# Clearing a block's semaphores from GpSimd inside the next block, without the second meeting of all engines at three inner block ends

## What is computed

```
x = x + 0.5 * ffn(layernorm(x))
x = x + attn(layernorm(x))
x = x + 0.5 * ffn(layernorm(x))

def ffn(x):                          # soft mixture of experts, 16 experts with 64 slots each
    x  = layernorm(x) * g + b
    se = (layernorm(slot_embeds) * slot_g + slot_b) * scale
    logits   = einsum('bnd,esd->bnes', x, se)
    dispatch = softmax(logits, axis=1)             # over tokens
    combine  = softmax(logits over all e*s)        # over slots
    slots = einsum('bnd,bnes->besd', x, dispatch)
    gate  = gelu(slots @ Wg + bg);  up = slots @ Wu + bu
    eout  = (gate * up) @ Wd + bd
    return einsum('bns,bso->bno', combine, eout)

def attn(x):                         # linear attention inside chunks of 32 tokens
    Q, K, V = x@Wq.T, x@Wk.T, x@Wv.T
    S = einsum('bncd,bnkd->bnck', Q, K) * decay_mask
    O = einsum('bnck,bnkd->bncd', S, V)
    return sigmoid(x@Wg.T) * O @ Wo.T + x
```

## Time and profile before

| | |
|---|---|
| median of 3 runs | 1861.09 us (1861.06 to 1861.68) |
| the profiled execution, its own time | 1854.48 us |
| its span, first to last instruction | 1852.8 us |
| TensorE busy | 1800.0 us, 97% of the span, 11756 matmuls |
| VectorE, ScalarE, GpSimd busy | 71%, 63%, 45% |
| mean granted TensorE clock | 0.998 |

### The profile page before, as it was taken

The page is one execution under the profiler, slowest core; times in us unless marked ns, Lnnn a source line. Parts: engine busy times, 40 slices in busy tenths (PEclk is TensorE's granted clock), DMA queues, the critical chain, the costliest instruction groups (busy, mean ns, idle before and its releaser), DMA issues. The chain is left out here.

```text
span 1852.8 us, 35562 instructions
## 1 busy us (share of the span) xinstructions
PE 1800.0 (97%) x11756; PEld 1620.4 (87%) x11756; DVE 1309.5 (71%) x2365; ACT 1161.3 (63%) x2285; POOL 825.1 (45%) x1036
## 2 busy tenths in 40 slices
PE   6999999999999999999999999999999999999998
PEld 5788888878999999989999877888888789999998
DVE  6866666664899888855555587666565668997886
ACT  5776676675665777754444367666666755667774
POOL 3423334234788655422222134242432458885553
PEclk9999999999999999999999999999999999999999
DMA  4642443251654777712222165333323426647773
GB/s 156 233 151 100 159 158 119 108 192 36 221 195 156 254 268 267 285 47 69 68 68 68 58 238 193 120 142 147 148 102 114 159 88 230 204 173 269 262 257 146
DMA packets 106940, 297.85 MB, mean 161 GB/s; under 512 B 16784, under 2 KB 56592, under 8 KB 94544
## 3 DMA queue, kind: packets, MB, share of 16 engines
q1 hardware_dynamic: 106832, 296.49, 44.7%
HBM read 187.18 MB, written 109.28 MB: 160 GB/s over the span
## 5 line engine op out<-in xcount | busy, mean ns | idle before, releaser
L115 POOL TENSOR_TENSOR pool_carrier<-minus_half 128x1 f32<-128x1 f32 x224 | 71.7, 320 | 599.5 <-PE f2bank L984 197.6
L824 ACT ACTIVATE f2r_lt<-f2bank,slot_shift 128x512 f32<-128x512 f32 x128 | 88.3, 690 | 125.3 <-PE f2bank L955 125.2
L824 ACT ACTIVATE f1r_lt<-f1bank,slot_shift 128x512 f32<-128x512 f32 x128 | 88.3, 690 | 122.1 <-PE f1bank L955 122.0
L673 DVE TENSOR_TENSOR f2r_e_lo<-f2bank,f2r_e_hi 128x512 fp32r<-128x512 f32 x128 | 82.4, 685 | 80.6 <-ACT f2r_e_hi L905 80.6
L673 DVE TENSOR_TENSOR f1r_e_lo<-f1bank,f1r_e_hi 128x512 fp32r<-128x512 f32 x128 | 82.4, 684 | 79.7 <-ACT f1r_e_hi L905 79.7
L1685 PE MATMUL f1bank<-f1c_eo,f1c_e_hi 128*128 128x258 f32 (+1 forms) x512 | 130.6, 287 | 0.5 <-DVE f1c_xout L1591 0.4
L1685 PE MATMUL f2bank<-f2c_eo,f2c_e_hi 128*128 128x258 f32 (+1 forms) x512 | 130.0, 286 | 0.5 <-DVE f2c_xout L1591 0.4
L1686 PE MATMUL f1bank<-f1c_eo,f1c_e_hi 128*128 128x256 f32 (+1 forms) x512 | 128.2, 282 | 0.0
L1686 PE MATMUL f2bank<-f2c_eo,f2c_e_hi 128*128 128x256 f32 (+1 forms) x512 | 128.1, 282 | 0.0
L1538 POOL TENSOR_TENSOR f1c_e_lo<-f1c_lt,f1c_e_hi 128x512 fp32r<-128x512 f32 x64 | 82.7, 1294 | 76.7 <-ACT f1c_e_hi L1651 76.7
L1538 POOL TENSOR_TENSOR f2c_e_lo<-f2c_lt,f2c_e_hi 128x512 fp32r<-128x512 f32 x64 | 82.8, 1295 | 75.7 <-ACT f2c_e_hi L1651 75.7
(11 more groups left out here) (347 smaller groups left out, 6661.2 us busy)
## 6 DMA issues: line engine op xcount, KB each, us to landing
logits<-f1r_lt SPq DMA_DIRECT2D x16, 2048.0 KB, 7.3
f1c_lt<-logits SPq DMA_DIRECT2D x32, 1024.0 KB, 7.3
logits<-f2r_lt SPq DMA_DIRECT2D x16, 2048.0 KB, 7.3
f2c_lt<-logits SPq DMA_DIRECT2D x32, 1024.0 KB, 7.0
normalized<-t_xin SPq DMA_DIRECT2D x32, 512.0 KB, 2.6
t_xin<-in_L_attn_x SPq DMA_DIRECT2D x16, 512.0 KB, 5.1
f1r_xback<-normalized SPq DMA_DIRECT2D x16, 512.0 KB, 8.1
f1e_raw_g<-in_L_ffn_Wg SPq DMA_DIRECT2D x16, 512.0 KB, 3.9
```

What stands on the lines that cost most here:

```text
L115: pool.tensor_tensor(c["pool_carrier"][:, col:col + 1], c["minus_half"][:, 0:1], c["minus_half"][:, 0:1], ALU.add)
L673: dve.tensor_tensor(e_lo[t % 2][:, h * BANK:(h + 1) * BANK], ps_t[h][:, :], rd(e_hi[t % 2][:, h * BANK:(h + 1) * BANK]), ALU.subtract).the ...
L824: act.activation(lt[:, g, sc, :], ps_l[sc % 2][:, :], ACT.Identity, bias=c["slot_shift"][:, sc:sc + 1]).then_inc(logit_out, 1)
```

## The change

At the three inner block ends (setup to f1, f1 to attention, attention to f2) the scope no longer clears its semaphores and no longer calls the second meeting. `leave` empties the scope's list, the stage function returns the semaphores, and the next block's GpSimd program clears them with `clear_left`: in a feed-forward block as the first thing GpSimd does, in the attention block also first, ahead of its two counts and of `residual(0, 0, True)`. Because the numbers are freed only while the next block is written, the next block gets others: 103 to 142 for the setup, 143 to 255 for f1, 103 to 138 for the attention, 143 to 239 for f2. To have enough of them, the setup gives up one: `both_done` is folded into `gain_step`, for whose value 5 TensorE now waits. The ends of f2 and of the whole kernel keep the clear and the second meeting.

```diff
@@ -72,6 +72,17 @@
             self.nc.clear_and_free_semaphores(self.sems)
             self.nc.all_engine_barrier()
 
+    def leave(self):
+
+        left, self.sems = self.sems, []
+        return left
+
+
+def clear_left(nc, left):
+
+    if left:
+        nc.clear_and_free_semaphores(left)
+
 
 class Stage:
 
@@ -199,7 +210,7 @@
         ps_shift = banks[KD * HB + KD + 1]
         emb_loaded = [al.sem(f"emb_loaded{i}") for i in range(4)]
         columns_loaded, bias_loaded = al.sem("columns_loaded"), al.sem("bias_loaded")
-        const_done, ident_zero, gain_step, both_done = (al.sem(n) for n in ("const_done", "ident_zero", "gain_step", "both_done"))
+        const_done, ident_zero, gain_step = (al.sem(n) for n in ("const_done", "ident_zero", "gain_step"))
         stats_done, mv_done, var_done, rstd_done = (al.sem(n) for n in ("stats_done", "mv_done", "var_done", "rstd_done"))
         emb_done, shift_mm, all_out, shift_done = (al.sem(n) for n in ("emb_done", "shift_mm", "all_out", "shift_done"))
         tr_done, plain_done, weights_done, hi_done, lo_done = (
@@ -209,6 +220,7 @@
         ld_loaded, z_step, a_step, steps_done, mask_done, mask_stored = (
             al.sem(n) for n in ("ld_loaded", "z_step", "a_step", "steps_done", "mask_done", "mask_stored"))
         tokens = first_tokens(al, c, "next_", tk, prm["x"], tokens_tr)
+        left = al.leave()
         units = [(h, k) for h in range(HB) for k in range(KD)]
         PER = NSC // 4
         block = ctx.enter_context(nc.Block())
@@ -261,7 +273,7 @@
             pool.tensor_tensor(gains[:, :], scaled_gain[:, :], columns[:, 0, :], ALU.mult).then_inc(gain_step, 1)
             pool.tensor_tensor(offsets[:, :], scaled_gain[:, :], columns[:, 1, :], ALU.mult).then_inc(gain_step, 1)
             for i in range(2):
-                pool.tensor_tensor(both[:, i, :], columns[:, i, :], c["shift"][:, :], ALU.mult).then_inc(both_done, 1)
+                pool.tensor_tensor(both[:, i, :], columns[:, i, :], c["shift"][:, :], ALU.mult).then_inc(gain_step, 1)
 
             pool.wait_ge(a_step, 3)
             blocks = mask[:, :].rearrange("p (c i) -> p c i", i=CHUNK)
@@ -338,7 +350,7 @@
                 mm = pe.transpose(small[:, i * E * KF:(i + 1) * E * KF], bias_rows[:, i, :],
                                   c["ident"][0:E * KF, 0:E * KF])
             mm.then_inc(bias_tr, 1)
-            pe.wait_ge(both_done, 2)
+            pe.wait_ge(gain_step, 5)
             for sc in range(NSC + 1):
                 if sc % (NSC // HB) == 0 and sc < NSC:
                     pe.wait_ge(plain_done, KD * (sc // (NSC // HB) + 1))
@@ -1874,7 +1888,7 @@
                           normalize, weights, weights_hi, weights_lo, transpose, tokens_hi, tokens_lo)
 
 
-def attention_stage(nc, c, tag, pl, x_in, x_stored, x_out, stored, tk):
+def attention_stage(nc, c, tag, pl, x_in, x_stored, x_out, stored, tk, left):
 
 
 
@@ -1895,6 +1909,7 @@
          xT_lo_done, xT_out, q_mm, q_out, gate_mm, gate_done, v_mm, v_out,
          s_mm, s_masked, o_mm, o_gated, o_hi_done, o_lo_done, y_mm, y_done) = (al.sem(n) for n in names)
         tokens = first_tokens(al, c, "next_", tk, x_out, ps_q)
+        leave = al.leave()
         block = ctx.enter_context(nc.Block())
 
         def groups(eng, emit):
@@ -1946,6 +1961,7 @@
                     pool.wait_ge(y_done, KD * (g - 1))
                 pool.tensor_tensor(base[q][:, :, :], xin[q][:, :, :], xn[q][:, :, :], ALU.add).then_inc(base_done, 1)
 
+            clear_left(nc, left)
             for s in (var_done, rstd_done):
                 pool.sem_inc(s, 1)
             residual(0, 0, True)
@@ -2165,6 +2181,8 @@
             pe.wait_ge(y_done, KD * (NGR - 1))
             rows(ps_t, o_hi, o_lo, "o", y_mm)
 
+    return leave
+
 
 FirstExpert = namedtuple("FirstExpert", "load_first first_gate_up first_gate_lo first_up_lo first_down first_in_hi first_in_lo second_gate_up second_gate_lo")
 FirstGroup = namedtuple("FirstGroup", "load_first make_ones first_shifts first_spread")
@@ -2176,7 +2194,7 @@
 FirstTokens = namedtuple("FirstTokens", "load all_loaded statistics scale normalize transpose hi lo")
 
 
-def feed_forward(nc, c, tag, prm, tk, x_in, x_stored, x_out, stored, scratch, attention=None):
+def feed_forward(nc, c, tag, prm, tk, x_in, x_stored, x_out, stored, scratch, left, attention=None):
 
     with ExitStack() as ctx:
         al = Scope(nc, ctx, tag)
@@ -2192,6 +2210,7 @@
                                                 scratch["max_rows"])
         r_programs = route_stage(c, route, tk, banks, first_expert, x_in, x_stored, slots, neg_row_max, scratch["logits"],
                                  scratch["normalized"], scratch["inverse"])
+        leave = al.leave() if attention else []
         block = ctx.enter_context(nc.Block())
 
         @block.sync
@@ -2242,10 +2264,10 @@
         first, second = token_places(al, "t1_"), token_places(al, "t2_")
         attention = attention_places(al, "at_")
         a_stored, b_stored = ([al.sem(f"{n}_stored{i}") for i in range(2)] for n in "ab")
-        setup_stage(nc, c, prm, scratch["mask"], first)
-        feed_forward(nc, c, "f1", prm, first, prm["x"], (), x_a, a_stored, scratch, attention)
-        attention_stage(nc, c, "at_", attention, x_a, a_stored, x_b, b_stored, second)
-        feed_forward(nc, c, "f2", prm, second, x_b, [(s, 1 + B * NG // 2 * DMA) for s in b_stored], out, None, scratch)
+        left = setup_stage(nc, c, prm, scratch["mask"], first)
+        left = feed_forward(nc, c, "f1", prm, first, prm["x"], (), x_a, a_stored, scratch, left, attention)
+        left = attention_stage(nc, c, "at_", attention, x_a, a_stored, x_b, b_stored, second, left)
+        feed_forward(nc, c, "f2", prm, second, x_b, [(s, 1 + B * NG // 2 * DMA) for s in b_stored], out, None, scratch, left)
 
 
 # ---- launch: one core; inputs and outputs as the reference has them ----
```

## The result

| | before | changed |
|---|---|---|
| median of 17 runs each, same conditions | 1860.7 us | 1856.15 us |
| lowest and highest | 1855.41 to 1863.59 | 1852.99 to 1859.69 |
| ratio, 95% interval | | 0.9980 (0.9973 to 0.9987) |
| span of the profiled execution | 1852.8 us | 1852.3 us |
| mean granted TensorE clock, profiled execution | 0.998 | 0.998 |

The change makes the kernel 3.7 us faster by the ratio (2.4 to 5.0 us), 4.5 us by the medians. 0.4 us of this is the base: the median of before is 1860.7 us over 17 runs, and was 1861.09 over the three at hand. The 17 runs of before also show what the three runs at hand did not: one kernel's executions differ by 8 us.

The account below looks back on a forecast made before the run. TensorE, busy 97% of the span, was taken to bound the kernel. Gains of 0.45 (setup's end), 0.25 (f1's end) and 0.65 us (attention's end) summed to 1.35 us off 1861.09, giving 1859.7 us; range 1857.6 to 1861.5.

Parts of the forecast that it names:

- The second meeting's share of each pause: Part of TensorE's pauses at the setup's, f1's and attention's ends due to the second meeting: 0.7, 1.15 and 0.65 us.
- The clears hidden in f1 and f2: At the starts of f1 and f2, VectorE's statistics cover GpSimd's clears with drains, 0.4 us each; costed at nothing.
- The chain at the attention's start: GpSimd, VectorE and TensorE form one chain to group 1's transposes; the clear at its head costs 0.9 us.
- rival 3: At block starts engines do not start earlier, as the next block's instructions arrive late; no change, 1861.1 us; chance 0.17.
- rival 4: GpSimd's clear at the attention's start is slowed by other engines' counting; at ten times its time 1865.6 us; chance 0.06.
- rival 2: In the attention a later TensorE wait covers GpSimd's clear; 2.25 us less in all, 1858.8 us; chance 0.08.
- the one on TensorE's clock: Around the attention's end one half-clock stretch still follows either pause, so no gain from its absence is counted.
- the rival's 1.6 us: The half-clock stretch near f2's start goes, 1.6 us more gained; 2.95 us less in all, 1858.1 us; chance 0.24.
- the direct sum: Gains from earlier starts at the setup's, f1's and attention's ends: 0.45, 0.25 and 0.65 us, together 1.35 us.
- the slow stretch in f1: Sign of being right: the half-clock stretch at f1's start ends about where it did, 25.9 us, with more products.
- Whether the start of f1 gains 0.45 or 0.7 us: At the setup's end, 0.45 us if the slow stretch's end stays at 25.9 us, 0.7 if it moves with the work.

Follow-up runs that it names:

- the kept meeting: Changed kernel with the second meeting put back at the three inner block ends, GpSimd's clear staying in the next block; ratio to before 1.0002 (0.9992 to 1.0012).
- the second profile: The kernel before, unchanged, profiled once more on the third chip; span 1864.3 us at a mean clock of 0.993.

## Why the prediction was wrong

**Right.** The second meeting's share of each pause (0.7, 1.15, 0.65 forecast; 0.69, 1.18, 0.64 measured). The clears hidden in f1 and f2: GpSimd's first wait there still ends by VectorE, after 11.78 and 23.10 us. The chain at the attention's start, its link, its place and its price (0.9 forecast, 0.88 measured), confirmed by moving the clear behind it. No late instructions (rival 3), no slowing of the clear by the other engines (rival 4), no cover for the chain (rival 2).

**Wrong.** The step that failed is the one on TensorE's clock: "I take it that one slow stretch still follows, after either pause". It set the clock's gain at nothing and gave its going 0.24. What happened is more than the rival's 1.6 us, for two reasons that the runs show. First, the pause ahead of the attention counted too. The profile read had no slow stretch there, and I took its pause of 2.94 us for one that the clock survives; over five profiles with this pause it did not in three, and not behind the kept meeting's pause of 2.06 us either. Second, shortening to 1.7 us is enough in every one of the eight profiles, which I could not read from one. The clock's term, put at 0, is 2.8 us by the count over the profiles, and 2.9 us by the clocks of the timed runs; both are estimates, and each is twice the direct sum. The range failed with it: its lower end took in one slow stretch less and 0.5 us. A sign of being right failed too: the slow stretch in f1 was to end about where it did, and ended 1.9 us later, at 27.8.

**What should have been a warning.** The profiled execution lay 6.6 us below the median, and the text carried this difference over "unchanged" as something that nothing in the trace shows. Most of it was the clock: the profiled execution had a mean of 0.998, before's runs on the first chip 0.9942, and 0.0038 at 1.5 us per 0.001 are 5.7 us. The trace read was before's lucky case, with one slow stretch after f1's start, where the second profile had five.

**Open.** Whether the start of f1 gains 0.45 or 0.7 us: the slow stretches around the setup's tail are 3.4, 6.8 or 10.2 us long from profile to profile, and TensorE ends the setup anywhere from 21.5 to 24.2 us, which covers it. The run with only the setup's end changed shows no gain (1.0005). Why only the attention's end brought 0.7 us by the ratio, and not 2.4, is not settled either; its interval, 2.8 less to 1.3 more, holds both. What decides between two runs of one program whether a pause of 2.2 us is followed by a slow stretch was not tried. And the estimate by the clock lies above what was measured for 7 of the 11 kernels, for the changed one by 1 us (4.3 and 3.2), so the size of the clock's share is known to about 1 us only.

## What to carry to other kernels

A meeting of all engines costs more than the time between its releases: it lengthens TensorE's pause, and a pause that is a few tenths of a microsecond too long can bring a half-clock stretch worth 1.3 to 1.9 us behind it; here a kept meeting of 0.3 us at each end undid the whole gain, where the meetings' own time is 1.0 us of it. Unread products can fill such a pause, but they have to end before the other engines reach the meeting: 14 of them, 3.3 us, made the next block start 1.7 us later. When bookkeeping moves off the meeting and onto one engine, put it behind that engine's first critical result, not at the head of its program: the same clear cost 0.9 us less one helper further on. And when a profiled execution is faster than the median by more than the effect to be judged, compare their granted clocks before reading anything from it.

## What the runs showed of the hardware

- Pauses of TensorE of 1.86 to 3.24 us were followed by 3.4 us at the lower clock level in 26 of 36 cases, pauses of 1.4 to 1.81 us in 0 of 49. The Trainium skill (TensorE: Matmul & The Clock Gate, HAM oscillation — how this bites in real kernels) gives as the rule to avoid idle gaps above a length that all of these pauses keep under; the traces do not agree, shorter pauses were enough here in 26 of 36 cases. The Trainium skill (TensorE: Matmul & The Clock Gate, Part 1: The HAM clock gate) says that the gate's timing is free-running and does not start anew with the kernel. This fits the traces, in which the same pause of 2.94 us has the stretch behind it in three profiles and not in two.
- Between the timed runs of one program the mean granted clock goes from 0.993 to 0.996 on two chips and from 0.990 to 0.996 on the third, with 1.5 to 1.6 us for each 0.001.
- A range clear on GpSimd takes 222 to 224 ns for 36 semaphores, 248 and 265 ns for 40 and 41, 655 ns for 113, the same whether the other engines stand still or count beside it.
- Products that nobody reads, put where TensorE would stand still, kept its clock up: mean 0.9966 against 0.9938 of before, and a ratio of 0.9985 (0.9973 to 0.9997), where the same kernel without them has 0.9946 against 0.9941 and 1.0002 (0.9992 to 1.0012) on another chip. Where they outlast the other engines' work they delay the meeting: 1.67 us for 14 of them.
